# Rows of a four-layer block on one core: finer pieces in every turn, turns without a loop, and the last experts in batches of eight tiles

## What is computed

```python
x = x + mamba2_twice(ln(x))            # two state-space blocks over the 1024 positions
x = x + ffn0(ln(x))                    # 8 small MLPs, weights from a softmax over the mean
x = x + einsum_layer(ln(x), acc1)      # log-space products, per row of the image
x = x + moe1(ln(x))                    # 8 experts, top 2
x = x + einsum_layer(ln(x), acc2)
x = x + lstm(ln(x))                    # 1024 steps in sequence, 8 sequences
x = x + conv7x7_attention(ln(x))       # depthwise 7x7, ReLU, BN, softmax attention over 1024 positions
x = x + moe2(ln(x))                    # 8 experts, top 2, gates renormalised; its own input ln(x) added too
```

## Time and profile before

| what | value |
|---|---|
| median of 3 runs | 3486.21 us (3484.66 to 3487.12) |
| profiled execution | 3478.68 us, its span 3476.9 us |
| mean granted TensorE clock | 0.789 |
| busy in the span | TensorE 82%, VectorE 61%, ScalarE 49%, GpSimd 22% |

### The profile page before, as it was taken

One profiled execution on the slowest core, in us unless ns is written; L12 is line 12 of the kernel. 1 busy time (PEld: TensorE's weight loads), 2 busy tenths in 40 slices (PEclk: granted clock), 3 DMA queues, 4 the chain that ended last, 5 costly groups with the idle time before them and its releaser, 6 DMA issues. The chain is left out here.

```text
span 3476.9 us, 72552 instructions
## 1 busy us (share of the span) xinstructions
PE 2849.0 (82%) x22302; PEld 2325.8 (67%) x22302; DVE 2121.4 (61%) x8884; ACT 1696.4 (49%) x5788; POOL 766.8 (22%) x1419
## 2 busy tenths in 40 slices
PE   4477888898888888889898888889888669887675
PEld 3365666677777777777777777777777554555565
DVE  4566566666666666666666666666644322556777
ACT  1254555555565565555555555555555322443232
POOL 2233222222222222222232222222211000000100
PEclk9687666688787888888888877877867669998677
DMA  2000000000010000000000000000000000000000
GB/s 92 12 16 16 16 17 17 17 18 19 19 31 18 18 18 18 18 18 17 18 17 18 19 19 23 26 18 17 17 16 8 3 16 11 1 1 3 8 7 8
DMA packets 53970, 59.73 MB, mean 17 GB/s; under 512 B 26448, under 2 KB 45008, under 8 KB 53200
## 3 DMA queue, kind: packets, MB, share of 16 engines
q1 hardware_dynamic: 53584, 54.98, 5.3%
HBM read 42.35 MB, written 4.19 MB: 13 GB/s over the span
## 5 line engine op out<-in xcount | busy, mean ns | idle before, releaser
L1116 DVE TENSOR_TENSOR_SCAN r_c<-r_wk 64x24 f32<-64x24 f32 x1024 | 272.6, 266 | 588.8 <-ACT r_wk L1102 576.9
L1091 PEld LDWEIGHTS psL<-r_h,lv 128*64 128x64 f32 x2048 | 244.7, 164 | 509.7 <-DVE r_h L1121 372.8
L1091 PE MATMUL psL<-r_h,lv 128*64 128x8 f32 x2048 | 324.3, 231 | 304.1 <-DVE r_h L1121 271.7
L1102 ACT ACTIVATE r_wk<-psL 64x16 f32<-64x16 f32 x1024 | 189.4, 185 | 688.2 <-PE psL L1092 674.0
L1196 PE MATMUL psL<-img,dg 128*128 (+1 forms) x2744 | 439.9, 318 | 1.1 <-DVE r_h L1121 1.1
L1196 PEld LDWEIGHTS psL<-img,dg 128*128 128x128 f32 x2744 | 399.0, 226 | 6.3 <-issue 1.2
L1107 ACT ACTIVATE r_tc<-r_c 64x8 f32<-64x8 f32 x1024 | 217.2, 212 | 277.0 <-DVE r_c L1116 223.6
L1093 PE MATMUL psL<-r_h,lv 128*64 128x8 f32 x2048 | 330.2, 234 | 0.0
L1092 PE MATMUL psL<-r_h,lv 128*64 128x8 f32 x2048 | 308.2, 223 | 0.0
L1121 DVE SCALAR_TENSOR_TENSOR r_h<-r_wk,r_tc 64x8 f32<-64x8 f32 x1024 | 187.3, 183 | 138.2 <-ACT r_tc L1107 128.9
L1092 PEld LDWEIGHTS psL<-r_h,lv 128*64 128x64 f32 x2048 | 257.7, 174 | 0.0
(11 more groups left out here) (407 smaller groups left out, 6709.0 us busy)
## 6 DMA issues: line engine op xcount, KB each, us to landing
accb<-acc_in SPq DMA_DIRECT2D x64, 512.0 KB, 3.5
a_xy<-a_E SPq DMA_DIRECT2D x512, 16.0 KB, 1.8
W<-pack_in SPq DMA_DIRECT2D x1, 3165.0 KB, 14.1
x6d<-X SPq DMA_DIRECT2D x64, 32.0 KB
out_x<-X SPq DMA_DIRECT2D x32, 64.0 KB, 1.6
X<-x_in SPq DMA_DIRECT2D x1, 1856.0 KB, 18.1
W<-pack_in SPq DMA_DIRECT2D x1, 1331.0 KB, 5.6
X<-x_in SPq DMA_DIRECT2D x1, 192.0 KB, 6.2
```

The lines of the kernel that those rows point to most:

```text
L1091: nc.tensor.matmul(psL[0:64, par, c:c + LB], lv[:, 0], h, start=False, stop=False, skip_group_check=True)
L1102: nc.scalar.activation(o, psL[0:64, par, c:c + 2 * LB].rearrange("p (g b) -> p g b", b=LB), ACT.Tanh).then_inc(sem("r_gi"), 1)
L1116: v.tensor_tensor_scan(r_c3[:, t % 2, :], r_wk[:, 0:24], r_wk[:, 30:54], 0.0, ALU.mult, ALU.add).then_inc(sem("r_c"), 1)
```

## The change

1. **Pieces split.** Generators yield more often (some 60 new yields): convolution taps two at a time (before: runs of up to 11), the state-space blocks' matmuls, copies and vector steps singly, the expert matmuls and activations singly. `TIMES` is new for all engines.
2. **Turns written out.** The loop is gone; all turns are straight code with constant semaphore values.
3. **Edge.** Rows 27 to 31 of the convolution leave the row-wise part and stage 2. In turns 31 and 32 `edge_pe` adds up rows 28 to 31 in one PSUM bank of `psA` and row 27 in the other.
4. **Last experts.** Stage 4 is written anew: batches of eight tiles for norm, logits and gates; pairs of tiles in three PSUM banks for the experts; the sum over experts as a tree of adds on GpSimd; the bias of the second expert layer by one matmul a batch.

```diff
             act.wait_ge(ve, V.at(i, "y"))
             for j in range(J):
+                if j:
+                    yield
                 last = nc.scalar.activation(u["T"][:, j * DI:(j + 1) * DI], u["y"][:, j], ACT.Square, accum_out=u["ss"][:, j:j + 1])
...
-                for ky, kx in TAPS[n:n + count]:
+                for c, (ky, kx) in enumerate(TAPS[n:n + count]):
+                    if c and c % 2 == 0:
+                        yield
                     last = nc.tensor.matmul(o, dg[:, ky * KT + kx], rows[:, :, ky, kx:kx + IMG], start=(n == 0), stop=(n == KT * KT - 1))
...
-            with eng.Fori(FIRST_FULL, LAST_FULL, 2) as i:
-                turn(i, FIRST_FULL % 2)
-                turn(i + 1, (FIRST_FULL + 1) % 2)
-            for i in range(LAST_FULL + 1, NT + 1):
+            for i in range(FIRST_FULL, NT + 1):
                 turn(i, i % 2)
 # TIMES, rows of block0 and block1 on three engines (ACT: the 7th of 9 entries and the 11th of 14 is Yv)
-        (0, 2, 4, 4, 8, 10, 23, 27, 29),                                   # ACT block1
-        (2, 5, 8, 8.5, 10, 13, 20, 25, 30),                                # ACT block0
+        (0, 0, 2.5, 3, 6, 6, 6, 6, 7, 10, 15, 26.5, 27.5, 29),
+        (3, 3, 5, 5, 8, 8, 8, 9, 10.5, 13, 17.5, 27, 27, 30),
-        (0, 1, 2, 3, 4, 5, 10, 11, 11.5, 15.5, 16.5, 25, 26, 31.5),         # DVE block1: y2 at 26
-        (2.5, 4.5, 5.5, 7, 8, 9.5, 11, 13, 14.5, 15.5, 18.5, 20.5, 23, 28), # DVE block0: y2 at 23
+        (0, 0, 0, 2, 2, 3, 3.5, 4, 4.5, 4.5, 5, 5.5, 6, 6, 8, 8, 8.5, 10, 10.5, 11, 12.5, 12.5, 25, 25.5, 26, 31, 31), # y2 at 25.5
+        (3, 3, 3, 4, 4.5, 5, 6.5, 7, 7.5, 8, 8.5, 8.5, 9, 9.5, 10.5, 11, 11.5, 13.5, 13.5, 15, 16.5, 16.5, 18.5, 23.5, 26.5, 27.5, 27.5), # y2 at 23.5
 # TIMES, convolution on PE: 12 runs of (11,1,7,3,2,1,3,2,1,6,8,4) taps, then 28 of one or two
-        (0, 7, 9, 9, 11, 13.5, 14.5, 15.5, 15.5, 15.5, 17, 18),
+        (0, 0, 0, 0.5, 0.5, 7, 8.5, 8.5, 9.5, 10, 11, 11, 12, 13.5, 15.5, 16, 16.5, 16.5, 16.5, 18, 18, 18, 18, 18.5, 18.5, 19.5, 20, 21),
+        def edge_pe(pe, n):
+            if n == 0:                                  # turn 31
+                pe.wait_ge(sem("x6_free"), NT - 2)
+                for t in range(2 * KT):
+                    yield 2 + t
+                    edge(t // KT, t % KT, 0, 4, start=(t == 0), stop=False, skip_group_check=True)   # 512 columns
+                    for ky, kx in TAPS[3 * t:3 * t + 3]:
+                        row27(ky, kx)                                                               # 128 columns
+            else:                                       # turn 32
+                yield 22
+                for kx in range(KT):
+                    if kx == 3: yield 30.5
+                    last = row27(KT - 1, kx)
+                    for ky in range(2, 6):
+                        edge(ky, kx, 0, 6 - ky, start=False, stop=False, skip_group_check=True)                    # 512, 384, 256, 128 columns
+                yield 31.5
+                pe.wait_ge(sem("x6_free"), NT)
+                for kx in range(KT):
+                    for r in range(4):
+                        last = edge(6 - r, kx, r, r + 1, start=False, stop=(kx == KT - 1 and r == 3), skip_group_check=True)
-                for n, (ky, kx) in enumerate(TAPS):     # stage 2
-                    last = nc.tensor.matmul(o, dg[:, n], img[:, :, LAST_ROW + ky:LAST_ROW + ky + NEW, kx:kx + IMG],
-                                            start=(n == 0), stop=(n == KT * KT - 1))
 # stage 4, order on VectorE and on TensorE; u is a pair of tiles, n = u // 4 the batch, r = u % 4
+                for u in range(NU2):                    # VectorE
+                    if r == 0 and more: moments(n + 1)
+                    if u: product(u - 1)
+                    if r == 0 and more: norm(n + 1)
+                    if r == 1:
+                        bias(n)
+                        if more: skip(n + 1)
+                    if r == 2 and more: logits(n + 1)
+                    if r == 3 and more: gates(n + 1)
+                for u in range(NU2):                    # TensorE
+                    first(u)
+                    if u: second(u - 1)
+                    if r == 0: turn_gates(n)            # waits for gates(n)
+                    if r == 0 and more: turn(n + 1, 0)  # waits for norm(n + 1)
+                    if r == 1:
+                        if more: turn(n + 1, 1)
+                        biases(n)
+                    if r == 2 and more: logits(n + 1)
+            def tree(u):                                # GpSimd
+                for c, k in enumerate((4, 2, 1)):
+                    g.tensor_tensor(big[:, :, 0:k], big[:, :, 0:k], big[:, :, k:2 * k], ALU.add)
+                g.tensor_tensor(XN[:, J * u:J * u + J], e_z[n % 2][:, r:r + J], big[:, :, 0], ALU.add)
```

More of the change, by code:

```diff
@@ L1229, in weave @@
                     while due <= slot:
-                        due = next(g, None)
+                        new = next(g, None)
+                        due = due if new == SAME else new
                         if due is None:
@@ L1752, in _ @@
+                for u in range(NU2):
+                    sp.wait_ge(sem("done"), u + 1)
+                    sp.dma_start(o_v[:, J * u:J * u + J, :], XN[:, J * u:J * u + J, :]).then_inc(sem("out"), 16)
+                sp.wait_ge(sem("out"), NU2 * 16)
             @block.gpsimd
             def _(pool):
[L1754 to L1756 removed]
+                g = nc.gpsimd
@@ new lines, in _ @@
+                v.memset(e_m8[:], -0.5)
+                v.memset(e_eps[:], 1e-5)
+                v.memset(e_g[:], NEG)
+                v.memset(e_rep[:], NEG)
+                for k in (0, 1):
+                    last = v.memset(e_xT[k][64:P], 0.0)
+                last.then_inc(sem("zeroed"), 1)
+                dve.wait_ge(sem("zeroed"), 1)
+                moments(0)
+                norm(0)
+                skip(0)
+                logits(0)
+                gates(0)
+                for u in range(NU2):
+                    n, r = divmod(u, PER)
+                    more = n + 1 < NBAT
+                    if r == 0 and more:
+                        moments(n + 1)
+                    if u:
+                        product(u - 1)
+                    if r == 0 and more:
+                        norm(n + 1)
+                    if r == 1:
+                        bias(n)
+                        if more:
+                            skip(n + 1)
+                    if r == 2 and more:
+                        logits(n + 1)
+                    if r == 3 and more:
+                        gates(n + 1)
@@ new lines, in logits, with turn_gates @@
+                def logits(n):
+                    pe.wait_ge(sem("xTs"), 2 * n + 2)
+                    if n:
+                        pe.wait_ge(sem("cwTs"), n)
+                    xT = e_xT[n % 2][:].rearrange("p u t -> p (u t)")
+                    for g in range(G):
+                        last = nc.tensor.matmul(psG[:, g * E:(g + 1) * E], xT[:, g * P:(g + 1) * P], w128("m2gate"), start=True, stop=True)
+                    last.then_inc(sem("lg"), 1)
+                def turn_gates(n):
+                    pe.wait_ge(sem("cw"), n + 1)
+                    nc.tensor.transpose(psG[0:G * E, P:2 * P], e_cw[n % 2][:].rearrange("p g e -> p (g e)"), ident).then_inc(sem("cwT"), 1)
@@ new lines, in biases, with first @@
+                def biases(n):
+                    pe.wait_ge(sem("cwTs"), n + 1)
+                    pe.wait_ge(sem("xTs"), min(2 * n + 4, 2 * NBAT))
+                    nc.tensor.matmul(psT, e_cwT[:], e_b2[:].rearrange("p g c -> p (g c)"), start=True, stop=True).then_inc(sem("bres"), 1)
+                def first(u):
+                    n, r = divmod(u, PER)
+                    ps = pairs_ps[u % 3]
+                    if u > 2:
+                        pe.wait_ge(sem("big"), u - 2)
+                    for q in range(4):
+                        last = nc.tensor.matmul(ps[:, q // 2, (q % 2) * 256:(q % 2 + 1) * 256], w128("m2w1", q * P, (q + 1) * P), e_xT[n % 2][:, r],
+                                                start=True, stop=True)
+                        if q % 2:
+                            last.then_inc(sem("mm1"), 1)
@@ new lines, in second @@
+                def second(u):
+                    ps = pairs_ps[u % 3]
+                    pe.wait_ge(sem("h"), 2 * u + 2)
+                    for j in range(J):
+                        for q in range(4):
+                            last = nc.tensor.matmul(ps[:, j, q * P:(q + 1) * P], e_h[u % 2][:, q, j * P:(j + 1) * P], w("m2w2", q * P, (q + 1) * P),
+                                                    start=True, stop=True)
+                    last.then_inc(sem("y"), 1)
+                turn(0, 0)
@@ new lines, in _ @@
+                turn(0, 1)
+                logits(0)
+                for u in range(NU2):
+                    n, r = divmod(u, PER)
```

(16 more changed lines are left out.)

439 lines of the change are left out of this document (263 added, 176 removed), and 16 rows, old and new, of the table TIMES.

## The result

The changed kernel takes 3163.41 us (median of 4 runs, 3158.86 to 3168.29) against 3485.43 of the kernel before (3481.66 to 3487.12): ratio 0.908, 95% interval 0.906 to 0.910. That is 322 us less. The prediction was 3331, some 155 less, and its range ended at 3240: the direction was right, the size half of what came.

The account below looks back on a forecast made before the run. It took LSTM steps, lengthened by work standing ahead of LSTM instructions on their engines, to bound the turns. Terms summed to -154.7 us on 3478.7, giving 3324.0, or 3331 as median; range 3240 to 3425.

Parts of the forecast that it names:

- loop: Turns 5 to 26: writing them out removes ten loop jumps of 2.35 us each, -23.5 us, at no known cost.
- DMA wait: VectorE's wait before adding the moved result goes: -82.0 us in the looped turns, -11.2 in turns 0 to 4.
- finer pieces, new slots: Split pieces: zero for full turns (bounds -66 and +66 us), -12 for turns 28 to 31.
- edge: Turn 31 +13 us, LSTM's end to attention -21, attention's start +3; together -5 us (-15 to +12).
- last experts: Stage 4: 33.4 us a batch against 36.3 a pass; -21 us (bounds -52 and +10).
- the ring: Stage 4: TensorE and VectorE wait for each other in turn, 27.8 us a batch and some 1 us in hand-overs.
- The clock's part: Stage 4: TensorE stands about 10 us a batch and its clock falls behind that, +4.5 us a batch.
- the moved stall: Rival, chance 0.20: half-slot waits between scan and h take all 93 us the DMA gave; 3424 us.
- The clock holds: Rival, chance 0.13: TensorE pauses less, all full turns like the better one, 3 us more off each of 22; 3265 us.
- The pace of the busiest engine: Rival, chance 0.10: stage 4 runs at TensorE's 18 us a batch and ends 100 us sooner; 3231 us.
- GpSimd and VectorE do lengthen each other: Rival on their shared port, chance 0.05: VectorE waits out GpSimd's adds, stage 4 gets 40 us longer; 3371 us.
- new wait: Rival of a slower kernel, chance 0.04: in-order waits at VectorE's slots 26.5 to 28.5 in every full turn; 3507 us.

Follow-up runs that it names:

- e1: The kernel before with the looped turns written out and the same pieces and slots: 3445.8 us, ratio 0.992.
- e4: The changed kernel with every part of a split piece at the slot the whole piece had before: 3380.7 us, ratio 0.974.
- e5: The changed kernel with ScalarE's copy of block0's result at slot 20.5 instead of 17.5: 3282.0 us, ratio 0.944.
- e10: The changed kernel with only the convolution's taps in their old runs of up to 11, at the slot of their first two: 3342.2 us, ratio 0.961.
- e7: The changed kernel with TensorE's split pieces alone issued whole, at the slot of their first part: 3294.9 us, ratio 0.948.
- e11: The changed kernel with VectorE's split pieces alone issued whole, at the slot of their first part: 3396.8 us, ratio 0.976.
- e3: The kernel before with VectorE's add of the moved result later, block0 at slot 24.5 (was 23), block1 at 26.5 (was 26): 3451.6 us, ratio 0.995.
- e12: The changed kernel with last experts' moments and norm made for the batch after next, at r = 1 and r = 2: 3083.2 us, ratio 0.886.
- e6: The changed kernel with split pieces on all engines issued whole, at the slot of their first part: 3509.6 us, ratio 1.011.
- e9: e1 with four of block0's eight DMAs issued by GpSimd at slot 20 instead of by SyncE: 3414.1 us, ratio 0.982.

## Why the prediction was off

| term | predicted | found | from |
|---|---|---|---|
| loop | -23.5 | -38 (by the ratio -26) | e1 against before, spans |
| DMA wait | -93 | -113 to -123 | waits of e4 less those of the changed kernel; e5 against it, last h |
| finer pieces, new slots | -12 | -104 to -94 | e4 less the changed kernel, 217, less the line above |
| edge | -5 | -25 | last h to attention: -26.5; last h of e4 against e1: +2 |
| last experts | -21 | -38 | stage 4, 296 to 257.7 |
| sum | -155 | -318 | spans: -319.8 |

**The step that failed** is "Finer pieces. I take zero for full turns". The count behind it took, for each step, the TensorE work due in its slot beyond 1 us, and found 22 us a turn before and 21 after; the runs have 46 to 60 us in the 22 turns, 2.1 to 2.7 a turn. The same count on e10's slots, with the same durations, gives 2.0 us a turn more than on the changed kernel's, and the chip gives 7.0; for e7 it gives 1.5 and the chip 5.3. So the count ranks these orders rightly and is too small by a factor of three. What it leaves out is not settled. It treated each step by itself and each engine by itself, and it took one duration for each matmul, while TensorE's busy time grows by 4.2 us a turn in e10. For VectorE's half slots the prediction counted 8.2 us a turn before and 8.6 after, while e11 shows 9.1 us a turn from VectorE's pieces. Of the 94 us that e5 leaves, 46 are in the full turns (6.4 a turn between e4 and the changed kernel, 140, less the 94 that e5 has there; 60 by e4's own waits), inside the stated bound of 66; 29 are in turns 1 to 4; of the others some 10 are in turns 27 to 31 (15 with the wait's part) and 10 before turn 1. For turns 1 to 4 the prediction had no term at all but the wait.

**DMA wait:** right in mechanism. The chain stands in the changed kernel without a wait in full turns, and e5 shows the wait worth its whole length. It was too small since the 67 us of waits before the LSTM starts were not read, and 21 of them went as well: in all the waits fell by 116 us, from 162.2 to 46.3. e5 has 9 more.

**Loop:** the jumps were right to 2 us; the cost inside the turns was missing, 3 to 15 us in the old order.

**Edge:** turn 31 went from 59.7 to 62.0 us, but the new slots are in that too. With the old ones (e4) it is 65.5 against 60.1 (e1): the 14 pieces cost 5.4 us instead of 13, and the finer pieces gave 3.5 of it back (3 forecast). Attention did not start slower (271.1 to 270.5). The rest, 67.4 to 40.9, was forecast as 47. TensorE was through 25.9 us after the last h, where the prediction had 22 to 29, though it took 49 edge matmuls in turn 32 and the code has 56.

**Experts:** the ring was read rightly: VectorE 13.3 us from the product to the norm's end (12 forecast), TensorE 17.4 from there to the next product (20 forecast). The clock's part was too large: the first experts 3.37 instead of 1.97 us and the turn 1.06 instead of 0.60 make 1.9 us, not 4.5. So 30.7 a batch, not 33.4. VectorE's 13.3 us hold 2.4 beside GpSimd: the norm 3.50 us instead of 1.88, and a product of the gates (L1883) 1.03 where one of the same size (L1894) takes 0.23.

**Rivals:** the moved stall did not come (e3 shows what it looks like). "The clock holds" is half right: 0.85 after 0.82, and turns alike, but e5 has 0.84 and 77.0 us. That it comes out near the found turn (81.0 less 1.1, 3.7 and 3 is 73.2; found 72.7) is luck: TensorE's busy time in these turns fell by only 10 us in all, from 1579.7 to 1569.6. The pace of the busiest engine was a matter of order alone: e12 has it. GpSimd and VectorE do lengthen each other (below), in the turns about as much before the change as after: VectorE's time beyond the quickest tenth of each kind of instruction is 135 us in the full turns before and 143 after. In stage 4 it is the 2.4 us a batch, some 15 us and not 40. No new wait stood ahead of h.

## What to carry to other kernels

Here a serial chain that shares in-order engines paid for the long runs ahead of its instructions: split the long runs (here the taps, and VectorE's pieces) and spread their parts. Neither does it alone: split pieces at the old slots gave nothing (e4), and whole pieces at the new ones cost 6.6 us a turn against e1 (e6). Compare orders on the chip, since a count per slot gave the sign and a third of the size of e7 and e10. A wait for a transfer cost three quarters of what it shows or all of it when it stood on that chain, and is taken away by starting the transfer earlier, not by moving its user a step. When two engines wait for each other in turn, walk the ring once on paper: here two moves of moments and norm, with what hangs on them, were worth 80 us.

## What was not expected of the hardware

VectorE's instructions of the chain grow when GpSimd works at the same time. e11, timeline:

```profile
1287.63 2.44 POOL L678 TENSOR_TENSOR a_xw<-a_S,a_dtm 128x512 f32<-128x512 f32 x2 [5.14 <-DVE a_dtm L591]
1288.07 1.01 DVE L1077 SCALAR_TENSOR_TENSOR r_h<-r_wk,r_tc 64x8 f32<-64x8 f32 x1
1289.12 0.98 DVE L1079 SCALAR_TENSOR_TENSOR r_wk<-r_h,r_c 64x8 f32<-64x8 f32 x1
```

As a rule they take 0.16 and 0.17 us. In stage 4 the norm of eight tiles takes 1.88 us with GpSimd idle and 3.50 beside its adds. The Trainium skill (SBUF — State Buffer, "SBUF: two separate sides") has it that GpSimd and a VectorE instruction with two inputs in SBUF, or in a mode that takes both ports, lock each other out for the whole length of an instruction. The two rows of the chain, with two such inputs each, agree: each ends within 0.02 us of one of GpSimd's two (1289.07 and 1290.08).

One DMA issue on SyncE takes 0.7 us here, so the sixteen of two blocks take as long as six LSTM steps (changed kernel, timeline). A second queue takes part of that off (e9):

```profile
1225.79 10.80 SPq L699 DMA_DIRECT2D a_xy<-a_E  x16
```
